# Attention and feed-forward block on one core: value products of two key tiles placed together, and the causal mask of half of the diagonal maximum slots added by TensorE

## What is computed

```
q = qkv[..., :512].reshape(B, S, 32, 16)
k, v = qkv[..., 512:528], qkv[..., 528:]
scores = einsum('bqhd,bkd->bhqk', q, k) * 16 ** -0.5
scores = where(pos_k <= pos_q, scores + slopes * (pos_k - pos_q), -1e30)
attn = einsum('bhqk,bkd->bqhd', softmax(scores), v)
x = x + attn @ Wo
x = x + ffn(layernorm(x))      # base product, top-2 of 8 experts of rank 16
```

## Time and profile before

| what | us |
| --- | --- |
| median of 3 runs (lowest, highest) | 790.23 (788.66, 791.53) |
| span of the profiled execution | 788.3 |
| up to the turn at the end of step 1 | 192.95 |
| steps 2 to 15, from turn to turn | 401.74 |
| step 16 and the feed-forward part | 193.6 |

### The profile page before, as it was taken

One profiled execution on the slowest core, in us unless ns is written; L12 is line 12 of the kernel. 1 busy time (PEld: TensorE's weight loads), 2 busy tenths in 40 slices (PEclk: granted clock), 3 DMA queues, 4 the chain that ended last, 5 costly groups with the idle time before them and its releaser, 6 DMA issues.

```text
span 788.3 us, 16078 instructions
## 1 busy us (share of the span) xinstructions
PE 691.0 (88%) x4224; PEld 299.5 (38%) x4224; DVE 576.1 (73%) x1851; ACT 356.9 (45%) x493; POOL 187.6 (24%) x340
## 2 busy tenths in 40 slices
PE   4486535989999999999999999999999996699997
PEld 2243212333344344344334334334433453355553
DVE  6175344989988988989898998898892372366664
ACT  2133010246676666676666666666666410011111
POOL 0010101132242242133233224224233311222221
PEclk9888677999999999999999999999999999699999
DMA  9559799111043052062061085500000189400001
GB/s 235 71 150 128 113 129 224 67 37 64 31 59 55 29 70 43 27 74 52 16 96 39 16 108 91 84 30 16 15 29 30 37 141 162 117 27 27 27 27 53
DMA packets 37592, 56.06 MB, mean 71 GB/s; under 512 B 6028, under 2 KB 19468, under 8 KB 37524
## 3 DMA queue, kind: packets, MB, share of 16 engines
q1 hardware_dynamic: 35468, 49.17, 35.1%
q0 software_dynamic: 1792, 6.29, 2.4%
q10 hardware_dynamic: 288, 0.07, 0.0%
HBM read 35.72 MB, written 19.79 MB: 70 GB/s over the span
## 4 chain that ended last, share of the span: by engine, by line
PE 67%; DMA 14%; DVE 11%; issue 4%; SPq 3%; ACT 1%; DVEq 0%; POOL 0%; POOLq 0%; ACTq 0%
PE psum L606 19%; PE psum L561 16%; PE psum L588 9%; PE psum L630 5%; PE psum L652 5%; DMA q_dram<-work 4%; PE psum L585 4%; DMA arena<-q_dram 4%; DMA x_sb<-in_x 4%; DVE psum L967 3%; PE psum L522 3%; DMA out<-wqkv_sb 3%; DVE negm L972 2%; PE psum L647 1%; PE psum L662 1%
## 5 line engine op out<-in xcount | busy, mean ns | idle before, releaser
L791 ACT ACTIVATE work<-psum 128x1024 f32<-128x1024 f32 (+1 forms) x320 | 289.7, 943 | 161.6 <-PE psum L588 136.2
L967 DVE CUSTOM_DVE_ANT_0 psum<-psum,future 128x384 f32<-128x384 f32 (+3 forms) x512 | 240.0, 517 | 33.1 <-PE psum L561 26.2
L561 PE MATMUL psum<-k_op,arena 106*128 106x512 bf16 (+3 forms) x768 | 209.5, 331 | 35.6 <-DMA arena<-q_dram 20.2
L972 DVE TENSOR_REDUCE negm<-psum 128x1 f32<-128x512 f32 x256 | 163.1, 684 | 29.1 <-PE psum L561 28.4
L606 PE MATMUL psum<-work,v_op 128*32 128x512 f32 (+3 forms) x1536 | 164.3, 500 | 0.4 <-POOL work L1152 0.4
L588 PE MATMUL psum<-arena,k_op 109*128 (+4 forms) x640 | 158.6, 316 | 1.0 <-ACT work L791 0.8
L1152 POOL TENSOR_SCALAR_AFFINE_SELECT work<-work 128x512 f32<-128x512 f32 x128 | 81.6, 637 | 276.5 <-ACT work L791 276.5
L561 PEld LDWEIGHTS psum<-k_op,arena 106*128 (+1 forms) x768 | 69.9, 97 | 192.7 <-issue 95.7
L522 PE MATMUL psum<-work,wqkv_sb 128*128 128x512 f32 (+1 forms) x160 | 83.1, 642 | 15.9 <-issue 15.2
L585 PE MATMUL psum<-arena,k_op 116*128 (+1 forms) x512 | 85.1, 221 | 0.0
L588 PEld LDWEIGHTS psum<-arena,k_op 109*128 109x128 bf16 x640 | 60.3, 98 | 35.7 <-ACT work L791 8.9
(11 more groups left out here) (84 smaller groups left out, 453.1 us busy)
## 6 DMA issues: line engine op xcount, KB each, us to landing
o_dram<-o_sb SPq DMA_DIRECT2D x32, 256.0 KB
q_dram<-work POOLq DMA_DIRECT2D x16, 384.0 KB, 3.1
arena<-q_dram SPq DMA_DIRECT2D x12, 512.0 KB, 17.8
arena<-q_dram SPq DMA_DIRECT2D x48, 128.0 KB, 5.9
arena<-o_dram SPq DMA_DIRECT2D x32, 128.0 KB, 8.9
arena<-rcp_dram SPq DMA_DIRECT2D x32, 128.0 KB, 9.4
out<-wqkv_sb SPq DMA_DIRECT2D x16, 256.0 KB, 2.0
x_sb<-in_x SPq DMA_DIRECT2D x3, 1024.0 KB, 9.0
```

Source lines behind the costliest of these rows:

```text
L561: last = nc.tensor.matmul(bank[:, a * width:(a + 1) * width], q_op[0:ROW_MAX, bass.ds(col, P)], k_op[0:ROW_MAX, b, k0:k0 + width], start=T ...
L791: nc.scalar.activation(probs[:, n % 4, heads * hp:heads * (hp + 1), 0:w], src, ACT.Exp).then_inc(exp_done, 1)
L967: last = nc.vector.tensor_tensor_reduce(keys, keys, future[:, CH - width:CH], -1.0, 3e38, ALU.add, ALU.min, negm[:, late, 0, j * QT + t:j ...
L972: nc.vector.tensor_reduce(dst, psum[:, idx % NSB, 0:len(js) * width].rearrange("p (a k) -> p a k", a=len(js)), AX_X, ALU.max, negate=True) ...
```

## The change

On PE both halves of a tile's scores now stand before any value product, and the value products of two tiles come after the second, odd tile. Slots are still spread in proportion between all pieces. In a diagonal slot of t = 0 or 1 a third matmul adds the triangle (`cmask`, through the identity `identb`) to both heads in PSUM, and DVE then reduces both heads with one plain maximum. Two small copies make `identb` and `cmask` once. ACT's and POOL's queues are as before.

```diff
+MASKED = (0, 1)
...
         if 1 <= k <= NK:
-            work.append((UH // HALVES[n] * w, ("scores", k - 1, (n, 0))))
-        m, v = (k - 1, n - LAG) if n >= LAG else (k - 2, n - LAG + NTI)
-        if 0 <= m < NK:
-            work.append((UH * (CH - TILES[v][2]), ("values", m, v)))
-        if 1 <= k <= NK and HALVES[n] == 2:
-            work.append((UH // 2 * w, ("scores", k - 1, (n, 1))))
+            work += [(UH // HALVES[n] * w, ("scores", k - 1, (n, hp))) for hp in range(HALVES[n])]
+        if n % 2:
+            for v in (n - 1 - LAG, n - LAG):
+                m, v = (k - 1, v) if v >= 0 else (k - 2, v + NTI)
+                if 0 <= m < NK:
+                    work.append((UH * (CH - TILES[v][2]), ("values", m, v)))
...
+                masked = kind == "diag" and t in MASKED
                 for a, j in enumerate(js):
                     col = unit_col(2 * k + late, j, i) + t * P
                     last = nc.tensor.matmul(bank[:, a * width:(a + 1) * width], q_op[0:ROW_MAX, bass.ds(col, P)],
                                             k_op[0:ROW_MAX, b, k0:k0 + width],
-                                            start=True, stop=True)
+                                            start=(a == 0 or not masked), stop=not masked)
+                if masked:
+                    last = nc.tensor.matmul(bank[:, 0:len(js) * width].rearrange("p (a k) -> p a k", k=width)[:, :, width - P:width],
+                                            identb[:], cmask[:, None, :].broadcast_to((P, len(js), P)), start=False, stop=True)
...
-                    if kind == "diag":
+                    if kind == "diag" and t not in MASKED:
...
+            dve.wait_ge(ident_in_sem, 16)
+            nc.vector.tensor_copy(identb[:], ident[:]).then_inc(mask_set, 1)
+            nc.vector.tensor_copy(cmask[:], future[:, CH - P:CH]).then_inc(mask_set, 1)
```

More of the change, by code:

```diff
@@ L218, in build @@
         future = sb("future", [P, CH])
+        identb = sb("identb", [P, P], BF16)
+        cmask = sb("cmask", [P, P], BF16)
         kmask = sb("kmask", [P, 3])
@@ L255, in build @@
         ones_set = sem("ones_set")
+        mask_set = sem("mask_set")
         x0_in = [sem(f"x0_in{t}") for t in range(QT)]
@@ L684, in _ @@
                     pe.wait_ge(c_in, 16 * N_C)
+                    pe.wait_ge(mask_set, 2)
                     pe.wait_ge(k_ready, 1)
```

## The result

The changed kernel takes 833.88 us (832.37 to 835.35, 4 runs), the kernel before 789.85 on the same chips: a ratio of 1.056, 95% interval 1.054 to 1.058. It is 44 us slower. The way was forecast, the size was not: 817 was 17 us short and 826 was the end of the range.

A forecast was written before the change was run, and what follows sets the result against it. PE was taken to set the pace, DVE close behind. A step went to 30.55 us, +1.85; fourteen steps +25.9, plus 0.6, 0.5 and -0.5 elsewhere, gave +26.5 and a forecast of 817 us, range 802 to 826.

The forecast's parts named there:

- the cycle of the score buffers: PE's score pieces: one reached sooner than 1.72 us after the start of the piece two before must wait.
- the nine waits: PE at S1a, S1b, S3, S5a, S5b, S6b, S7a, S9a, S9b: waits for score buffers, 3.64 us a step.
- the walk: One inner step gone through from S0a with trace prices, noting where PE comes too early for a score buffer.
- The copies' part: ACT's copies at S3 and S6b: they wait for value products and delay exponentials; PE waits 0.60 and about 0.70 us.
- Changes of kind: PE switching between bf16 and value products, 0.24 us in and out: two fewer a step, -0.48 us.
- Triangles: Eight slots a step get a 256-column matmul on PE, 0.11 us each with hidden weight loads: +0.85 us.
- A step without waits: PE in steps 2 to 15 before the change: slots, turns, scores and values, together 26.4 us.
- The other 2.3 us: Rest of the 28.70 us step before the change: PE's waits, mostly for DVE, of which some 0.15 stay.
- its milder: Case where PE loses 2.6 us a step instead of 3.64, slots bunching differently: +0.85 a step, 803 us; chance 0.15.
- heavier case: Same PE waits, and the triangles' weights do not load beside other work, +11 us: 828 us; chance 0.10.
- the faster one: Rival: PE's ACT waits fall where it would wait for DVE anyway; DVE's relief decides, -0.9 a step, 777 us; chance 0.07.
- no change: Rival: half of the 3.64 us of waits are absent, today's DVE waits pay the rest: 790 us; chance 0.06.

The follow-up runs named there:

- copies_later: Changed kernel with ACT's two copies of finished outputs moved one piece later, behind the exponentials of S1b and S5b; 813.7 us, ratio 1.031.
- short_exps: Changed kernel with exponentials of only the first half of each piece's queries, the other half left out; 797.6 us, ratio 1.011.
- old_short_exps: Kernel before the change with exponentials of only half of each piece, the other half left out; 788.0 us, ratio 0.999.
- order_only: Changed kernel without the triangles: the new order alone, diagonal slots masked by DVE as in the kernel before; 835.3 us, ratio 1.057.
- triangle_only: Changed kernel with the old order of scores and value products, keeping triangle on PE and plain maximum; 791.3 us, ratio 1.0027.
- two_pairs: Kernel before the change with V10 V11 between S0b and S1a and V8 V9 behind S11, each pair adjacent; 786.8 us, ratio 0.9955.

## Why the prediction was right in its mechanism and wrong in its size

**Right.** What bounds the kernel, and that the new order trips over the cycle of the score buffers. S1a, S1b and S5a start 1.72 us after the pieces of their buffers, to the hundredth, and in the step that I read seven of the nine waits come within 0.1 us of the walk. Over the fourteen steps PE's waits for ACT are 3.72 us a step, where 3.64 was worked out, and those for DVE 0.18, where 0.15 was left. The copies' part is confirmed by copies_later, the exponentials' by short_exps and old_short_exps. Changes of kind: 0.56 us a step were saved, -0.48 was forecast. Triangles: the product behind one starts 0.11 us after it where nothing waits (352.94 to 353.06), so 0.85 us as forecast, with hidden weight loads. DVE's plain reductions of 2 x 128 take 417 ns, and 2 x 256 take 0.69 us, as assumed; DVE is busy 12 us less in the stretch, where some 15 were forecast. The feed-forward part and the start moved by 1.4 us in sum, against +0.6.

**Wrong.** The step of the prediction that failed is the passage "A step without waits is ... Together 26.4. The other 2.3 us of 28.70 are waits, mostly for DVE". A step without waits took 27.36 us before the change: 23.26 of streams, 3.01 at changes of kind, 0.65 of small losses (0.006 us each at some 100 products) and 0.44 of larger losses for which no engine's work had to be waited for. Waits ahead of scores and slots were 1.34 us, not 2.3; another 0.09 of waits for DVE lies inside the 3.01. Since the change was costed as if all but 0.15 of the 2.3 us went, 0.96 us a step of PE's own time was taken off that no order gives back.

The forecast of a step was 26.4 - 0.48 + 0.85 + 3.64 + 0.15 = 30.55 us; measured 31.68, 1.13 more. By the table, the differences are these.
- The step without waits, 27.36 instead of 26.4: 0.96 us, 13 us in fourteen steps. This is nearly the whole error.
- Losses without a wait grew from 1.09 to 1.21 us, with eight more products a step: 0.12 us, 2 us in all. They were not in the sum.
- The nine waits for ACT: 3.72 instead of 3.64, 0.08 us. That this is so near is in part luck. S3 loses 0.74 and S6b 0.89 (mean of the steps) where 0.60 and 0.70 were worked out, since the copies start 0.21 us after the product behind V11 or V3 does and the walk had 0.06, and since PE reaches V11 later than in the walk. S1a (0.18), S9b (0.29) and S5b (under 0.05) lose 0.25 us less than the walk had, which pays most of it back.
- Waits for DVE: 0.18 instead of 0.15, 0.03 us.
- Changes of kind gave 0.08 more than forecast.

Together these make 1.11 of the 1.13 us. The range failed for the same reason: its milder and its heavier case vary the waits and the weight loads, and none varies the 26.4.

The rivals: the faster one and no change are excluded by order_only and triangle_only. The heavier one came out near in time, 828, but its mechanism, weight loads that do not hide, is not what happened. The page "ScalarE: Activation LUTs" of the Trainium skill, section "Rules for kernel authors", gives 1.15 us for the exponential as an estimate from its budget; the trace of the changed kernel has 1.03 again. The nearness of the measured time to the sum that the page's figure would give (817 and 15 us) is chance.

What stays open: what the losses of 0.05 us and more are for which nothing had to be waited (0.44 us a step before), and why two_pairs gains 3 us and not 6.7 in full. The table gives 0.34 and 0.11 us a step to losses at scores and slots, and no run took them apart.

## What to carry to other kernels

An engine at 65% of a stretch can still set its time: what counts is the distance in the waiting engine's queue between two uses of one buffer against the buffer's cycle (here 1.72 us), not the busy share. When a queue of one engine serves two others through small rings, an order that suits one may starve the other; here clustering saved 0.56 us a step in changes of kind and added 3.6 us of waits for ACT. And when the cost of a reorder is summed, time that is not explained by streams is not all wait: take the starts of all products, and look for each loss whether the buffer that it needs had only just come free. Only those losses, and the changes of kind, are what a change of order can win back.

## What the runs showed of the hardware

A change between bf16 products over the full array and float32 products in four column strips costs PE 0.24 us, 0.14 behind and 0.10 ahead (medians over steps 2 to 15 of either kernel), while two groups of such strips follow each other with 0.03 lost. A product that waits for an exponential starts 0.05 or 0.06 us after its end; one that waits for DVE, 0.06 or 0.14 us after. Two copies of 0.59 us in an in-order queue cost 1.3 us a step by their place alone (31.68 against 30.39 us), which is what the walk had for S3 and S6b together.
